# Linear attention's key-value sums in the merging stage: a cross product of tokens and keys instead of values

## The reference, cut to what matters

```python
qkv = (x @ W_qkv.T).reshape(B, N, 3, H, E)
q, k, v = (qkv[:, :, 0], qkv[:, :, 1], qkv[:, :, 2])
q_ = relu(q) + scale
k_ = relu(k) + scale
kv = einsum('bnhe,bnhf->bhef', k_, v)
k_sum = sum(k_, axis=1)
z = 1.0 / (einsum('bnhe,bhe->bnh', q_, k_sum) + EPS)
out = einsum('bnhe,bhef->bnhf', q_, kv) * z[..., None]
out = out.reshape(B, N, C) @ W_proj.T + b_proj
```

## Time and profile before

| | us |
|---|---|
| median of 3 runs | 3242.42 |
| lowest and highest | 3235.12, 3244.03 |
| span of the profiled execution | 3179.3 |
| median less span | 63.1 |
| TensorE busy in the span | 2868.6 |

### The profile page before, as it was taken

One profiled execution on the slowest core, in us unless ns is written; L12 is line 12 of the kernel. 1 busy time (PEld: TensorE's weight loads), 2 busy tenths in 40 slices (PEclk: granted clock), 3 DMA queues, 4 the chain that ended last, 5 costly groups with the idle time before them and its releaser, 6 DMA issues.

```text
span 3179.3 us, 46211 instructions
## 1 busy us (share of the span) xinstructions
PE 2868.6 (90%) x16081; PEld 1650.9 (52%) x16081; DVE 1667.8 (52%) x3712; ACT 1138.0 (36%) x2501; POOL 1497.0 (47%) x1471
## 2 busy tenths in 40 slices
PE   6999999988899989958999998999999999999828
PEld 3433566667667644437777764444533333444324
DVE  7633356578444442256777643442368888521361
ACT  3312422279222222345666542220045454331201
POOL 0565755578645538642333204544666666200004
PEclk9999999999999989988999999999999999999859
DMA  5400001120111224434445555211176676500504
GB/s 175 142 19 5 7 23 48 52 71 16 33 45 46 75 99 161 180 90 129 133 129 150 141 144 163 82 60 37 42 221 213 204 214 199 146 0 27 185 0 133
DMA packets 275816, 320.84 MB, mean 101 GB/s; under 512 B 155791, under 2 KB 193553, under 8 KB 275588
## 3 DMA queue, kind: packets, MB, share of 16 engines
q1 hardware_dynamic: 219540, 182.05, 18.6%
q0 software_dynamic: 51840, 134.60, 13.8%
q10 hardware_dynamic: 4208, 1.25, 0.2%
HBM read 215.22 MB, written 104.60 MB: 101 GB/s over the span
## 4 chain that ended last, share of the span: by engine, by line
PE 80%; DVE 7%; ACT 6%; issue 5%; DMA 2%; POOL 1%; SPq 0%; DVEq 0%; ACTq 0%; POOLq 0%
PE bank L1522 5%; PE bank L2737 5%; PE bank L708 4%; PE bank L2728 4%; PE bank L1301 4%; PE bank L2393 3%; PE bank L2909 3%; PE bank L2902 3%; PE bank L439 3%; PE bank L2137 2%; PE bank L731 2%; PE bank L2150 2%; PE bank L762 2%; PE bank L1117 2%; PE bank L2128 2%
## 5 line engine op out<-in xcount | busy, mean ns | idle before, releaser
L2708 POOL DMA_INDIRECT conv_src<-xn_rows,keep x288 | 290.4, 1009 | 140.8 <-issue 95.9
L291 POOL DMA_INDIRECT sorted_bias<-perf_rec,place x256 | 259.2, 1013 | 146.5 <-PE bank L708 92.1
L2737 PE MATMUL bank<-conv_msg,conv_hot 128*128 128x512 f32 x432 | 203.5, 594 | 0.0
L666 POOL DMA_INDIRECT sorted_edge<-rec,place x128 | 126.8, 990 | 141.7 <-PE bank L1362 75.2
L1933 POOL TENSOR_TENSOR delta_dec<-delta_dec,rates_of 128x512 f32<-128x512 f32 x64 | 66.5, 1039 | 253.3 <-ACT delta_dec L1985 253.3
L2788 DVE TENSOR_TENSOR conv_msg<-bank,conv_src 128x1024 f32<-128x1024 f32 x144 | 175.7, 1220 | 18.0 <-PE bank L2728 18.0
L1117 PE MATMUL bank<-bias_prod,bias_hot 128*128 128x256 f32 x640 | 148.2, 387 | 25.3 <-ACT bias_hot L1070 13.1
L2728 PE MATMUL bank<-conv_we,conv_eT 64*128 64x512 f32 x576 | 165.5, 652 | 1.1 <-ACT conv_eT L2762 1.1
L1101 POOL TENSOR_TENSOR bias_prod<-bias_col,bias_rec 128x512 f32<-128x512 f32 x128 | 147.2, 1179 | 16.6 <-PE bank L1117 15.8
L1117 PEld LDWEIGHTS bank<-bias_prod,bias_hot 128*128 128x128 f32 x640 | 120.2, 192 | 53.8 <-issue 28.2
L2766 ACT ACTIVATE conv_msg<-conv_msg 128x1024 f32<-128x1024 f32 x108 | 114.2, 1057 | 87.3 <-DVE conv_msg L2788 87.3
(11 more groups left out here) (508 smaller groups left out, 6794.2 us busy)
## 6 DMA issues: line engine op xcount, KB each, us to landing
keep<-slot_qkv SPq DMA_DIRECT2D x32, 512.0 KB, 4.7
delta_kv<-slot_qkv SPq DMA_DIRECT2D x32, 512.0 KB, 3.9
sorted_edge<-sort_pad SPq DMA_DIRECT2D x8, 1440.0 KB, 7.6
keep<-sorted_edge SPq DMA_DIRECT2D x18, 640.0 KB, 5.4
slot_out<-delta_o SPq DMA_DIRECT2D x64, 128.0 KB, 2.7
conv_src<-xn_rows,keep POOLq DMA_INDIRECT x288, 3.7
X<-in_x SPq DMA_DIRECT2D x4, 1024.0 KB, 11.1
sorted_bias<-perf_rec,place POOLq DMA_INDIRECT x256
```

The costliest lines, as they stand in the source:

```text
L291: POOL.indirect_dma_start(out=sorted_bias, out_offset=bass.IndirectOffsetOnAxis(ap=place[:, 0, c:c + 1], axis=0), in_=rec0[:, c, :], in_of ...
L2708: POOL.indirect_dma_start(out=src[:, n % 4, j, :], out_offset=None, in_=xn_rows, in_offset=bass.IndirectOffsetOnAxis(ap=rec[:, g % 3, k + ...
L2737: a = PE.matmul(bank[n % 2][:, :], hot[:, g % 2, k + j, :].bitcast(F32), msg[:, q, j, :], start=j == 0, stop=j == 1)
```

## The change

No values are formed. For each tile TensorE multiplies xn (as the stationary operand, in its 4 blocks) with k, and sums over the tiles in four PSUM banks ("cross"). VectorE adds up k over the tiles ("k sum"). At the end ScalarE and VectorE copy the four banks into wm's buffer (`by_key`), and TensorE multiplies them with the value weights, 16 calls of 128 columns; the sums of the keys come from 4 calls with 2 columns of ones. xn gets a third buffer, since the cross product reads it late; the projection keeps to one bank and waits for the add of the tile before; "k" moves to 2.62, behind "norm"; wv is loaded later.

```diff
-            xn = sb("xn", [P, 2, D])
+            XN = 3
+            xn = sb("xn", [P, XN, D])
-            va = sb("va", [P, 2, H, HV])
+            k_sum = sb("k_sum", [P, D])
+            by_key = wm
...
-                                 ("xnT", 2.1), ("K", 2.3), ("k", 2.55), ("V", 2.6), ("v", 2.9), ("kv", 3.3)):
+                                 ("xnT", 2.1), ("K", 2.3), ("k", 2.62), ("cross", 2.95), ("k sum", 2.97)):
...
-                SP.dma_start(wv[:, :, :], qkvT[:, :, 2 * D:3 * D]).then_inc(*wv_in.up(16))
                 for _, what, t in plan:
                     if what == "mix" and t == 2:
                         SP.wait_ge(*mixed.at(3))
                         SP.dma_start(wq[:, :, :], qkvT[:, :, 0:D]).then_inc(*late_in.up(16))
+                        SP.dma_start(wv[:, :, :], qkvT[:, :, 2 * D:3 * D]).then_inc(*wv_in.up(16))
...
-                            POOL.memset(va[:, :, :, HD:HV], 1.0).then_inc(*zeroed.up())
...
-                        if t >= 2:
-                            PE.wait_ge(*ended.at(t - 1))
+                        if t >= 1:
+                            PE.wait_ge(*ended.at(t))
                         for c in range(KC):
-                            a = PE.matmul(bank[1 + 4 * (t % 2)], oT[:, t % 2, c * P:(c + 1) * P], wm[:, c, :], start=c == 0,
+                            a = PE.matmul(bank[1], oT[:, t % 2, c * P:(c + 1) * P], wm[:, c, :], start=c == 0,
                                           stop=c == KC - 1)
...
-                    if what == "kv":
+                    if what == "cross":
                         PE.wait_ge(*k_ready.at(t + 1))
-                        PE.wait_ge(*v_ready.at(t + 1))
-                        for p_ in range(KC):
-                            at = p_ % 2 * 2 * HV
-                            a = PE.matmul(bank[6 + p_ // 2][:, at:at + 2 * HV], k[:, t % 2, p_ * P:(p_ + 1) * P],
-                                          va[:, t % 2, 2 * p_:2 * p_ + 2, :].rearrange("p h d -> p (h d)"),
-                                          start=t == 0 and p_ % 2 == 0, stop=t == NT - 1 and p_ % 2 == 1)
-                        a.then_inc(*kv_sum.up())
+                        for c in range(KC):
+                            a = PE.matmul(bank[4 + c], xn[:, t % XN, c * P:(c + 1) * P], k[:, t % 2, :], start=t == 0,
+                                          stop=t == NT - 1)
+                        a.then_inc(*crossed.up())
+
+                PE.wait_ge(*wv_in.at(16))
+                PE.wait_ge(*ended.at(NT))
+                PE.wait_ge(*k_summed.at(NT - 1))
+                for p_ in range(KC):
+                    PE.matmul(bank[1][:, 2 * p_:2 * p_ + 2], k_sum[:, p_ * P:(p_ + 1) * P], ones[:, 0:2], start=True, stop=True)
+                PE.wait_ge(*cross_held.at(2))
+                PE.wait_ge(*k_ready.at(NT))
+                for p_ in range(KC):
+                    part = slice(p_ * P, (p_ + 1) * P)
+                    for c in range(KC):
+                        a = PE.matmul(bank[3][:, part], by_key[:, c, part], wv[:, c, part], start=c == 0, stop=c == KC - 1)
+                a.then_inc(*kv_sum.up())
...
-                    if what == "v":
...
+                ACT.wait_ge(*projected.at(NT))
+                ACT.wait_ge(*crossed.at(NT))
+                for c in range(2):
+                    a = ACT.activation(by_key[:, c, :], bank[4 + c], AF.Copy)
+                a.then_inc(*cross_held.up())
...
-                        if t >= 2:
-                            DVE.wait_ge(*turned.at(t - 1))
-                            DVE.wait_ge(*shifted.at(t - 1))
-                            DVE.wait_ge(*begun.at(t - 1))
+                        if t >= XN:
+                            DVE.wait_ge(*turned.at(t - XN + 1))
+                            DVE.wait_ge(*shifted.at(t - XN + 1))
+                            DVE.wait_ge(*begun.at(t - XN + 1))
+                            DVE.wait_ge(*crossed.at(t - XN + 1))
...
                         if t >= 2:
-                            DVE.wait_ge(*kv_sum.at(t - 1))
+                            DVE.wait_ge(*crossed.at(t - 1))
...
+                    if what == "k sum" and t >= 1:
+                        DVE.wait_ge(*k_ready.at(t + 1))
+                        if t >= 2:
+                            DVE.wait_ge(*k_summed.at(t - 1))
+                        DVE.tensor_tensor(k_sum[:, :], k[:, 0, :] if t == 1 else k_sum[:, :], k[:, t % 2, :],
+                                          ALU.add).then_inc(*k_summed.up())
+                DVE.wait_ge(*crossed.at(NT))
+                for c in range(2, 4):
+                    a = DVE.tensor_copy(by_key[:, c, :], bank[4 + c])
+                a.then_inc(*cross_held.up())
+                DVE.wait_ge(*kv_sum.at(1))
                 DVE.wait_ge(*zeroed.at(1))
-                for p_ in range(KC):
-                    for j in range(2):
-                        half, at = slice(j * HD, (j + 1) * HD), (p_ % 2 * 2 + j) * HV
-                        a = DVE.tensor_copy(kv[half, p_, j, :], bank[6 + p_ // 2][half, at:at + HV])
+                for j in range(2):
+                    half = slice(j * HD, (j + 1) * HD)
+                    DVE.tensor_copy(kv[half, :, j, 0:HD],
+                                    bank[3][half, :].rearrange("p (c j d) -> p c j d", c=KC, j=2)[:, :, j, :])
+                    a = DVE.tensor_copy(kv[half, :, j, HD:HV], bank[1][half, 0:2 * KC].rearrange("p (c i) -> p c i", c=KC))
                 a.then_inc(*kv_ready.up())
```

More of the change, by code:

```diff
@@ L2268, in program @@
             (stats, aggregated, variance2, inverse2, normed, shifted, begun, turned, moved, eps_set) = of_norm = sig.several(10)
-            zeroed, k_done, v_done, k_ready, v_ready, kv_sum, kv_ready = of_sums = sig.several(7)
+            zeroed, k_done, k_ready, k_summed, crossed, cross_held, kv_sum, kv_ready = of_sums = sig.several(8)
             plan = []
@@ L2346, in pool @@
                             POOL.wait_ge(*stored[t % 2].at(16 * (t // 2)))
-                        POOL.tensor_tensor(xn_be[:, t % 2, :], xn[:, t % 2, :], be[:, :], ALU.add).then_inc(*shifted.up())
+                        POOL.tensor_tensor(xn_be[:, t % 2, :], xn[:, t % XN, :], be[:, :], ALU.add).then_inc(*shifted.up())
             late_banks = (bank[2], bank[3], bank[4], bank[7])
@@ L2382, in tensor @@
                         for c in range(KC):
-                            a = PE.transpose(bank[2][:, c * P:(c + 1) * P], xn[:, t % 2, c * P:(c + 1) * P], ident)
+                            a = PE.transpose(bank[2][:, c * P:(c + 1) * P], xn[:, t % XN, c * P:(c + 1) * P], ident)
                         a.then_inc(*turned.up())
-                    if what in ("K", "V"):
-                        i = what == "V"
+                    if what == "K":
                         PE.wait_ge(*moved.at(t + 1))
@@ L2388, in tensor @@
                         if t == 0:
-                            PE.wait_ge(*(wk_in, wv_in)[i].at(16))
+                            PE.wait_ge(*wk_in.at(16))
                         else:
-                            PE.wait_ge(*(k_ready, v_ready)[i].at(t))
+                            PE.wait_ge(*k_ready.at(t))
                         for c in range(KC):
-                            a = PE.matmul(bank[3 + i], xnT[:, c, t * P:(t + 1) * P], (wk, wv)[i][:, c, :], start=c == 0,
-                                          stop=c == KC - 1)
@@ L2395, in tensor @@
-                        a.then_inc(*(k_done, v_done)[i].up())
-                    if what == "kv":
+                            a = PE.matmul(bank[3], xnT[:, c, t * P:(t + 1) * P], wk[:, c, :], start=c == 0, stop=c == KC - 1)
+                        a.then_inc(*k_done.up())
+                    if what == "cross":
                         PE.wait_ge(*k_ready.at(t + 1))
-                        PE.wait_ge(*v_ready.at(t + 1))
-                        for p_ in range(KC):
-                            at = p_ % 2 * 2 * HV
-                            a = PE.matmul(bank[6 + p_ // 2][:, at:at + 2 * HV], k[:, t % 2, p_ * P:(p_ + 1) * P],
-                                          va[:, t % 2, 2 * p_:2 * p_ + 2, :].rearrange("p h d -> p (h d)"),
-                                          start=t == 0 and p_ % 2 == 0, stop=t == NT - 1 and p_ % 2 == 1)
-                        a.then_inc(*kv_sum.up())
+                        for c in range(KC):
+                            a = PE.matmul(bank[4 + c], xn[:, t % XN, c * P:(c + 1) * P], k[:, t % 2, :], start=t == 0,
+                                          stop=t == NT - 1)
+                        a.then_inc(*crossed.up())
@@ L2431, in scalar @@
                         ACT.wait_ge(*normed.at(t + 1))
-                        ACT.activation(acc[:, t, :], xn[:, t % 2, :], AF.Copy, scale=epsr[:, 0:1]).then_inc(*begun.up())
+                        ACT.activation(acc[:, t, :], xn[:, t % XN, :], AF.Copy, scale=epsr[:, 0:1]).then_inc(*begun.up())
                     if what == "xnT":
@@ L2436, in scalar @@
```

(33 more changed lines are left out.)

## The result

The changed kernel took 3262.95 us (median of 5 runs) where the kernel before took 3236.86 (median of 5). The ratio is 1.0057, with an interval of 1.0031 to 1.0084: 18 us slower, between 10 and 27. One of the five runs of the changed kernel took 15872.76 us, and such slow runs are left out of every ratio here, while the medians have them in. The two medians lie 26.1 us apart, which is inside the interval, near its upper end.

The account below looks back on a forecast made before the run. TensorE was taken to set the merging stage's pace, with VectorE's late row adding waits: 14 x 1.23 = 17.2 us plus 3.9 at the end, 21.1 on 3242.4, gave 3263.5 us; range 3252 to 3284.

Parts of the forecast that it names:

- K behind the second transposes: Merging tile, TensorE: without the key-value sums the xnT copy is uncovered, a 0.69 us hole; K starts at 1.29.
- The scale late: Merging tile: first transposes wait for VectorE's scale and start at 5.67 us, not 4.83; TensorE stands still 0.84.
- k behind the norm and the power: Merging tile: k waits for the norm and GpSimd's power, ends at 7.26 us; cross product starts at 7.31, 0.98 idle.
- The tile: Full merging tile: 7.31 + 3.54 cross + 3.46 projection = 14.31 us, 1.23 more than 13.08, 14 times: +17.2 us.
- The end: From the last second transposes to the last copy of the sums: 24.95 us instead of 21.05, +3.9 (3 to 7.5).
- The wait for the Square: VectorE's wait in each tile for ScalarE's Square, 7.0 us before; said to stay as before but longer.
- The parts of the old tile: Merging tile before the change: TensorE's groups, the 0.69 us hole and 0.04 between modelled ends said to add to 13.08.
- TensorE keeps the pace: Rival: VectorE's row is in time, k follows K's end, tile 12.75 us, about 3242 in all; chance 0.08.
- Faster: Rival: TensorE's groups run without any hole, 11.27 us a tile, 1.81 less, 3221 in all; chance 0.03.
- The clock: Rival: TensorE's clock falls after the holes in all 14 tiles, 1.7 us each, 24 us, 3287 in all; chance 0.07.
- GpSimd beside the k sum: VectorE's k sum, held by GpSimd up to 5.5 us, costs nothing; rival, norm held too: 19.6 us more, 3283, chance 0.04.
- Span and median: Whole kernel: the runs' median lies 63.1 us above the profiled span of 3179.3; left unchanged in the forecast.

Follow-up runs that it names:

- the Square first: Changed kernel with the Square of tile T+1 ahead of the xnT copy of T-1 on ScalarE's queue; ratio 0.9996 to the kernel before.
- the new order: Changed kernel with mix, Square, K, k, k sum and cross product moved so each copy and k lies beside a product; ratios 0.9938 and 0.9933 to the kernel before.
- k first: Changed kernel with k back at 2.55, ahead of the norm on VectorE's queue; ratio 1.0023 to the kernel before.

## Why the prediction was right

It said 3263.5 us, 21.1 more than before; 3262.95 was measured, and 18 (10 to 27) and 24 (15 to 32) us more. That the absolute time agrees to 0.6 us is luck: the 3242.4 that it started from became 3236.9 with two more runs, 5.6 too high, and its difference of 21.1 is 5.0 under the 26.1 of the medians. The two errors cancel. The mechanism is right in its steps, save one:

- **K behind the second transposes.** Said to start at 1.29 after them; it did at 1.28.
- **The scale late.** First transposes said at 5.67; measured 5.67. The idle time is 0.69 by the profile; the 0.84 of the prediction counted from where the next group could have started.
- **k behind the norm and the power.** Cross product said at 7.31; measured 7.31. Two experiments show the two causes apart: the Square first gives 12.74, k ahead of the norm 13.24.
- **The tile.** Said 14.31, measured 14.28; the projection is 3.43 from its start to the next group and not 3.46.
- **The end.** Said +3.9, measured +4.0.
- **The wait for the Square.** Said to be as before but longer; it was 4.19 us and not 7.01, because the k sum and the held multiply-add now lie ahead of it. It still ended when the Square did, so the path is as said.
- **The parts of the old tile.** As written, 0.44 + 0.90 + 6.92 + 0.45 + 0.69 + 3.54 + 0.04 is 12.98 and not 13.08; from the start of the first transposes to that of the projection it is 1.28 us (2104.57 to 2105.85), so what was put at 0.04 is 0.14. The forecast does not use this sum.
- **TensorE keeps the pace.** This rival's tile, 12.75, is the one that came (12.74) once the Square was put first, with its time of no change. It needs the row earlier, as said.
- **Faster.** 11.27 without holes was said; the new order has 11.18. The rival was right in size and needed another order.
- **The clock.** This is the step that was mis-sized. It stood as a rival with 0.07, at 14 falls and 24 us, and the forecast itself had no fall. There are falls in 4 of 14 tiles, 1.7 us each, 6.8 us in all: a term of the sum, not another case. The shorter hole did not protect every tile. With this term the sum would have been 27.9, and 3270.3 us from 3242.4. The range held it because it reached up to 3284.
- **GpSimd beside the k sum.** The row of 0.75 us was read as one beside no GpSimd work. GpSimd was on gathers (line 2319) from 1959.44 to 1960.48 and from 1960.79, and they did not hold that multiply-add, so the bound of 5.5 us counted them needlessly. The k sum was not held (0.69, beside a gather); the multiply-add behind it was, for 3.46 us, and ended 11.9 us after the second transposes, within the bound of 14.7. The conclusion, no cost, held; the norm took 0.59 and was not held, as the forecast had it. The Trainium skill (SBUF — State Buffer, section "SBUF: two separate sides") says that the loser is blocked for the whole instruction; in the timeline above the multiply-add lasted beyond GpSimd's shift and weighing both, so it was kept through more than one. The k sum of the kernel with the Square first shows the same (2.85 us): both ended 0.56 us after the weighing.
- **Span and median.** The 63.1 us were read as what lies around the span. Within one execution the two lie 1.9 us apart, and the rest is the difference between the session of the profile and that of the runs, as far as the sessions above tell. It did not spoil the sum, because only the difference was used.

## What to carry to other kernels

Removing a product from the engine that sets the pace also removes what it covered: ask of each copy and each wait which product lies beside it, before and after. A row of work on an engine that is half idle can still be late if its first instruction waits in another engine's queue; read where the row starts, not how much it is. With the same work, the place of the Square was worth 1.54 us a tile, and a full order without holes 3.1.

## What was not expected of the hardware

TensorE's clock fell in a stage where it is busy for 11.92 of 14.28 us and no single hole is over 1 us: the stretch of 0.69 idle, transposes and 0.98 idle comes in every tile, and in 4 of 14 tiles, in each of three profiles, the granted clock fell to 0.50 within some 1 us of the start of the product behind it. With a product of two instructions in the second hole (filled), or with that hole at nothing (k first), it did not happen; each of these was profiled once. Why it fell in those 4 tiles and not in the others stays open.

VectorE's multiply-add with inputs in SBUF took 3.46 us where it started 0.40 us before two GpSimd instructions that ran one behind the other (2070.58 to 2073.08), and 0.75 us in the orders where it stood free. Why it did not go first, though it started first, stays open; GpSimd was on a gather until 2070.57.

The same kernel took 3182 us in one session and 3231 to 3237 in three others. In its two profiles, of 3179.3 and 3238.0 us, the stage studied here has the same 13.08 us a tile.
